# First attention's tail, routing and slots run per batch between the heads of the next batch

## What is computed

```
logits = einsum('bsh,eh->bse', x, router_w) + expert_bias
scores = softmax(logits); top_w, top_idx = top_k(scores, 4)
top_w = top_w / sum(top_w)
out = sum over the four of top_w * down[e](silu(x @ gate[e]) * (x @ up[e]))
```

## Time and profile before

| | us |
|---|---|
| median of 3 runs | 710.92 |
| profiled execution | 710.83 |
| its span in the trace | 709.0 |
| TensorE busy | 551.6 (78%) |
| VectorE busy | 366.9 (52%) |
| ScalarE busy | 231.2 (33%) |
| GpSimd busy | 266.8 (38%) |
| mean granted clock of TensorE | 0.868 |

### The profile page before, as it was taken

How to read it: one execution, slowest core, us unless ns; L and a number is a source line. 1 busy time by engine, 2 the same in 40 slices (tenths; PEclk the granted TensorE clock), 3 DMA queues, 4 the chain that set the end, 5 groups by cost and what they waited for, 6 DMA issues and landing times.

```text
span 709.0 us, 10743 instructions
## 1 busy us (share of the span) xinstructions
PE 551.6 (78%) x3351; PEld 472.6 (67%) x3351; DVE 366.9 (52%) x956; ACT 231.2 (33%) x587; POOL 266.8 (38%) x243
## 2 busy tenths in 40 slices
PE   8889885000999999700488869669999999999994
PEld 5656574000898988600354438659999999999994
DVE  4554664500344444337479986596644444444445
ACT  4643523000455555501360103313333333333334
POOL 4462110376267894077118860040314124044000
PEclk9995987555899999955599996869999999999998
DMA  8942000122266775233100003001022020100001
GB/s 260 377 135 69 0 1 1 45 104 101 78 189 188 230 234 185 83 101 101 36 0 1 0 22 113 1 1 67 1 67 68 1 68 15 51 0 0 0 0 59
DMA packets 42266, 54.12 MB, mean 76 GB/s; under 512 B 5729, under 2 KB 37234, under 8 KB 42226
## 3 DMA queue, kind: packets, MB, share of 16 engines
q1 hardware_dynamic: 25330, 32.34, 14.5%
q10 hardware_dynamic: 13536, 12.33, 5.5%
q0 software_dynamic: 3360, 8.93, 3.9%
HBM read 36.02 MB, written 17.56 MB: 76 GB/s over the span
## 4 chain that ended last, share of the span: by engine, by line
PE 65%; DVE 11%; POOL 10%; issue 5%; DMA 4%; ACT 4%; POOLq 0%; ACTq 0%; SPq 0%; DVEq 0%
PE PS L1381 45%; POOL FA L629 4%; POOL xg L601 4%; PE PS L1577 3%; DMA FA<-xg 2%; PE PS L1478 2%; PE PS L1456 2%; DVE FA L1335 2%; PE PS L1612 1%; DVE PS L1319 1%; PE PS L1552 1%; PE PS L1636 1%; POOL FA L644 1%; PE PS L1441 1%; DMA FA<-in_w0T 1%
## 5 line engine op out<-in xcount | busy, mean ns | idle before, releaser
L1381 PE MATMUL PS<-EW,XH 128*128 128x384 f32 (+2 forms) x732 | 208.4, 366 | 6.0 <-DVE SQ L1169 4.4
L1381 PEld LDWEIGHTS PS<-EW,XH 128*128 128x128 f32 x732 | 126.2, 192 | 10.4 <-DVE SQ L1169 4.7
L1381 PE MATMUL PS<-EW,XL 128*128 128x384 f32 (+2 forms) x366 | 129.1, 353 | 0.0
L1169 DVE SCALAR_TENSOR_TENSOR SQ<-SIL,CW,PS 128x96 f32<-128x96 f32 x256 | 69.0, 311 | 115.7 <-ACT SIL L772 114.6
L1381 PE MATMUL PS<-EW,EHH 128*128 128x256 f32 (+1 forms) x476 | 101.7, 289 | 0.2
L772 ACT ACTIVATE SIL<-PS 128x192 f32<-128x192 f32 x128 | 42.6, 332 | 160.7 <-PE PS L1381 160.7
L1381 PE MATMUL PS<-EW,EHL 128*128 128x256 f32 (+1 forms) x286 | 80.1, 280 | 0.0
L1381 PEld LDWEIGHTS PS<-EW,EHH 128*128 128x128 f32 (+1 forms) x476 | 78.0, 188 | 1.1 <-issue 0.6
L1381 PEld LDWEIGHTS PS<-EW,XL 128*128 128x128 f32 x366 | 70.2, 192 | 2.2
L568 POOL TENSOR_TENSOR round_mark<-round_mark 128x1 f32<-128x1 f32 x10 | 2.2, 218 | 183.2 <-PE PS L1381 131.8
L1612 PE MATMUL PS<-ident,FA 128*128 128x128 f32 x94 | 19.0, 286 | 50.1 <-DMA FA<-xg 50.1
(11 more groups left out here) (294 smaller groups left out, 1098.3 us busy)
## 6 DMA issues: line engine op xcount, KB each, us to landing
EG<-in_gateup SPq DMA_DIRECT2D x16, 448.0 KB, 4.1
xg<-EQ SPq DMA_DIRECT2D x1, 6016.0 KB, 26.0
...
```

Of the source, the lines that this page charges most:

```text
L1169: ins = dve.scalar_tensor_tensor(out=HH[:, pos % 2, h:h + W], in0=SIL[:, s, j * W:(j + 1) * W], scalar=c, in1=bank(s)[:, I + j * W:I + (j ...
L1381: ins = pe.matmul(o, l, r, start=start and i == 0, stop=stop and i == n - 1, skip_group_check=True)
```

## The change

- The steps of a finished batch run between the heads of the next one, down to its slots. The numbers in the table (`COPY_AT`, ...) are units on ScalarE and VectorE and pairs of units on TensorE; `batch_at` adds 8 units or 4 pairs per batch. The loops run over 46 units.
- ScalarE copies the turned heads and their 17th-column sums (`copies`), the denominator is folded into the head norm (h/d normalised is h times an inverse root of var(h) + eps d d), and inverse roots are made on VectorE by `rsqrt` (an integer guess and three Newton steps, 10 instructions) in place of ScalarE's square root and a reciprocal.
- The router's weights are multiplied with the output projection once (`fold_transposes`, `fold_products`, `fold_router`), and stand as 16 more columns behind its 256 (DR = 272). The logits of x come from the same PSUM bank and are corrected with mean and deviation afterwards. The softmax of all 16 is gone: the exponential is taken of the four best only.
- An expert has a region of 1024 rows in `xg`, so that a slot is 1024 e + rank and needs no count of later batches. `xg` has 16384 rows. Its zeros are written by a DMA that ScalarE issues between its two tanh, where SyncE did it before. For each tile ScalarE reads the row at which it starts from a table in registers, 16 at a time (a load and 32 register instructions, at tiles 0, 16 and 32). The output tensor `yg` stays packed; `pack_slots` makes the second set of slots for its gather.
- GpSimd scatters batch by batch, 8 indirect DMAs each. The gates are made for two tiles at once.
- The copy of an output tile moves from ScalarE to VectorE (`outputs`).

```diff
-        xg = nc.dram_tensor("xg", (SLOT_TILES * P, D), F32).ap()
+        xg = nc.dram_tensor("xg", (E0 * T, D), F32).ap()
...
-        FLOOR_AT, EVAC_AT, TOKENS_AT = 2, 1, 4
-        HEADS_AT, SQUARE_AT, SUMS_AT = (4, 5), (5, 6), (6, 7)
+        ROWS_AT_ONCE = 16
+        FLOOR_AT, FOLD_COPY_AT, FOLD_AT = 2, 4, 8
...
+        EVAC_AT, COPY_AT, DEN_AT, SCALE_AT, PARTS_AT = 9, 12, 12, 13, 15
+        NORM_AT, X_AT, TOP_AT, PICK_AT, SLOT_AT = 17, 18, 18, 19, 21
+        TOKENS_AT, TURN_AT, PROJECT_AT, RANKS_AT = 5, 7, 8, 10
+        UNITS = (B - 1) * NH0 + SLOT_AT + 1
...
-            sp.wait_ge(zero_set, 1)
-            sp.dma_start(xg.rearrange("(n p) d -> p n d", p=P),
-                         EQ[:].rearrange("p t e -> p (t e)").unsqueeze(1).broadcast_to([P, SLOT_TILES, D])
-                         ).then_inc(xg_zero, 16)
...
-            for t in range(NT):
-                pool.wait_ge(hc_ready, t + 1)
-                pool.tensor_tensor(OGATE[:, t, :], OGATE[:, t, :], HC[:, t, :], ALU.mult).then_inc(og_ready, 1)
...
+            def gate(b):
+                two = slice(2 * b, 2 * b + 2)
+                pool.wait_ge(hc_ready, b + 1)
+                pool.tensor_tensor(OGATE[:, two, :], OGATE[:, two, :], HC[:, two, :], ALU.mult).then_inc(og_ready, 1)
+            def scatter(b):
+                pool.wait_ge(x_act, 2 * b + 2)
+                pool.wait_ge(slots_ready, b + 1)
+                for t in (2 * b, 2 * b + 1):
+                    for k in range(TOP0):
+                        n = t * TOP0 + k
+                        pool.indirect_dma_start(
+                            out=xg, out_offset=bass.IndirectOffsetOnAxis(ap=slots[:, n:n + 1], axis=0),
+                            in_=XB[:, t, :], in_offset=None).then_inc(scattered, 16)
+            gate(0)
+            gate(1)
+            pool.wait_ge(xg_zero, 16)
+            scatter(0)
+            gate(2)
+            scatter(1)
+            gate(3)
             split(BGH, BGL, bg[:]).then_inc(w_split, 1)
...
+            act.wait_ge(zero_set, 1)
+            act.dma_start(xg.rearrange("(n p) d -> p n d", p=P),
+                          EQ[:].rearrange("p t e -> p (t e)").unsqueeze(1).broadcast_to([P, E0 * NT, D])
+                          ).then_inc(xg_zero, 16)
...
+            def copies(b):
+                two = slice(2 * b, 2 * b + 2)
+                if b == 0:
+                    act.wait_ge(w_split, 4)
+                if b >= 2:
+                    act.wait_ge(sq_read, b - 1)
+                act.wait_ge(ao_tokens, 2 * b + 2)
+                ao = PS[:, 6:8, :].rearrange("p t (h v) -> p t h v", h=NH0)
+                act.activation(hn[:, two, 0:NH0], ao[:, :, :, DV0], ACT.Copy)
+                act.activation(HC[:, two, :].rearrange("p t (h v) -> p t h v", h=NH0), ao[:, :, :, 0:DV0], ACT.Copy
+                               ).then_inc(hc_ready, 1)
+                s = 2 * (b % 2)
+                act.activation(SQ[:, s:s + 2, :].rearrange("p t (h v) -> p t h v", h=NH0), ao[:, :, :, 0:DV0], ACT.Square
+                               ).then_inc(sq_done, 1)
...
+            def pair_x(b):
+                for t in (2 * b + 1, 2 * b):
+                    act.wait_ge(lg_ready, 2 * b + 1 + (t % 2 == 0))
+                    act.activation(XB[:, t, :], bank(7 - t % 2)[:, 0:D], ACT.Identity, bias=nb[:, t:t + 1],
+                                   scale=rstd[:, t:t + 1]).then_inc(x_act, 1)
...
+                if i % ROWS_AT_ONCE == 0:
+                    _, at = nc.values_load_multi_w_load_instructions(tile_rows[0:1, i:i + ROWS_AT_ONCE], engines=(mybir.EngineType.Activation,),
+                                        min_val=0, max_val=E0 * NT - 1)
+                    rows.update(enumerate(at, i))
+                act.dma_start(XG[:, i % 4, :], room[bass.ds(rows[i], 1)].rearrange("o p d -> p (o d)")
+                              ).then_inc(xg_ld[i % 4], 16)
...
+            def rsqrt(x, y, a, b):
+                ch.link(dve.tensor_scalar(y.bitcast(I32), x.bitcast(I32), -0.5, 1597463007.0, ALU.mult, ALU.add))
+                for _ in range(3):
+                    ch.link(dve.tensor_tensor(a, y, y, ALU.mult))
+                    ch.link(dve.scalar_tensor_tensor(out=b, in0=x, scalar=-0.5, in1=a, op0=ALU.mult, op1=ALU.mult))
+                    ch.link(dve.scalar_tensor_tensor(out=y, in0=b, scalar=1.5, in1=y, op0=ALU.add, op1=ALU.mult))
...
+            def scale_heads(b):
+                two = slice(2 * b, 2 * b + 2)
+                v, e2 = hs[:, two, 0:NH0], hs[:, two, NH0:2 * NH0]
+                dve.wait_ge(sq_done, b + 1)
+                s = 2 * (b % 2)
+                summed = dve.tensor_reduce(v, SQ[:, s:s + 2, :].rearrange("p t (h v) -> p t h v", h=NH0), AX_X, ALU.add)
+                summed.then_inc(sq_read, 1)
+                dve.wait_ge(sq_read, b + 1)
+                ch.link(dve.scalar_tensor_tensor(out=v, in0=v, scalar=NH0 / D, in1=e2, op0=ALU.mult, op1=ALU.add))
+                y = hr[:, two, 0:NH0]
+                rsqrt(v, y, hr[:, two, NH0:2 * NH0], e2)
+                dve.wait_ge(og_ready, b + 1)
+                shape = [P, 2, NH0, DV0]
+                dve.tensor_tensor(HC[:, two, :].rearrange("p t (h v) -> p t h v", h=NH0),
+                                  OGATE[:, two, :].rearrange("p t (h v) -> p t h v", h=NH0),
+                                  y.unsqueeze(3).broadcast_to(shape), ALU.mult).then_inc(gated, 1)
...
+            def pair_norm(b):
+                two = slice(2 * b, 2 * b + 2)
+                dve.wait_ge(y_done, 2 * b + 2)
+                for t in (2 * b + 1, 2 * b):
+                    ins = dve.bn_stats(st[:, t, :], bank(7 - t % 2)[:, 0:D])
+                ch.link(ins)
+                for t in (2 * b + 1, 2 * b):
+                    ins = dve.bn_aggr(mv[:, t, :], st[:, t, :])
+                ch.link(ins)
+                ch.link(dve.tensor_scalar(rv[:, two], mv[:, two, 1], EPS_LN, None, ALU.add))
+                rsqrt(rv[:, two], rstd[:, two], t1[:, two, 0], t1[:, two, 1])
+                ch.link(dve.scalar_tensor_tensor(out=nb[:, two], in0=mv[:, two, 0], scalar=-1.0, in1=rstd[:, two],
+                                                 op0=ALU.mult, op1=ALU.mult))
+                for t in (2 * b + 1, 2 * b):
+                    ins = dve.scalar_tensor_tensor(out=LG[:, t, E0:2 * E0], in0=wr0_sum[:], scalar=nb[:, t:t + 1],
+                                                   in1=bias_r0[:], op0=ALU.mult, op1=ALU.add)
+                ch.link(ins)
+                for t in (2 * b + 1, 2 * b):
+                    dve.scalar_tensor_tensor(out=LG[:, t, 0:E0], in0=bank(7 - t % 2)[:, D:DR], scalar=rstd[:, t:t + 1],
+                                             in1=LG[:, t, E0:2 * E0], op0=ALU.mult, op1=ALU.add).then_inc(lg_ready, 1)
...
+                def outputs(v):
+                    dve.wait_ge(tiles_done, v + 1)
+                    if v >= 4:
+                        dve.wait_ge(yg_st[v % 4], 16 * (v // 4))
+                    dve.tensor_copy(YO[:, v % 4, :], bank(6 + v % 2)[:, 0:D]).then_inc(y_evac, 1)
...
-            dve.wait_ge(w_split, 3)
-            layernorm(0, XB, y_done, lambda p: 2 * p + 2)
-            lo_parts(1, XL, XH)
-            softmax(0, E0, bias_r0[:])
-            dispatch()
-            normalise(t2, top, 4, None).then_inc(weights_ready, 1)
+            dve.wait_ge(slots_ready, B)
+            dve.tensor_tensor(t1[:, :, 0:TOP0], top[:, :, 0:TOP0], top[:, :, 0:1].broadcast_to([P, NT, TOP0]),
+                              ALU.subtract).then_inc(rt_max, 1)
+            tile_tables()
+            pack_slots()
+            dve.wait_ge(rt_exp, 1)
+            normalise(t2, t3, TOP0, None).then_inc(weights_ready, 1)
...
             def heads_to_tokens(b):
                 pe.wait_ge(ao_evac, 2 * (b + 1))
-                pe.wait_ge(at_ready, 2)
-                if b >= 1:
-                    pe.wait_ge(hc_ready, b * TB)
+                if b == 0:
+                    pe.wait_ge(fold_ready, 1)
...
+            def heads_turned(b):
+                pe.wait_ge(sq_done, b + 1)
+                pe.wait_ge(gated, b + 1)
+                for k in range(KD):
+                    for t in range(2):
+                        c = (k * 2 + t) * P
+                        ins = pe.transpose(bank(6)[:, c:c + P], HC[:, 2 * b + t, k * P:(k + 1) * P], ident[:])
+                ins.then_inc(tp_done, 1)
+            def project_pair(b):
+                if b == 0:
+                    pe.wait_ge(ld_x, 16)
+                else:
+                    pe.wait_ge(slots_ready, b)
+                pe.wait_ge(lo_done, b + 1)
+                for t in (2 * b + 1, 2 * b):
+                    o = bank(7 - t % 2)
+                    c = slice(t * P, (t + 1) * P)
+                    pe.matmul(o[:, 0:D], ident[:], XA[:, t, :], start=True, stop=True, skip_group_check=True)
+                    for k in range(KD):
```

(11 more changed lines are left out.)

370 lines of the change are left out of this document (232 added, 138 removed).

## The result

The kernel became slower: 717.81 us (median of 15 runs, 712.17 to 721.84) against 713.34 us for the kernel before (15 runs, 701.72 to 719.07). The ratio is 1.0139, with a 95% interval of 1.0106 to 1.0172. A second series gave 713.58 against 704.15 and 1.0137 (1.0075 to 1.0200). All ratios here leave out executions that took over 1.5% more than the fastest of their own kernel, which in the first series are eight of the 15 of the kernel before and none of the changed one, and so its two medians, taken of all, lie only 0.6% apart. The forecast was 695, and its range ended at 714. The loss is inside what the text called no change, but both intervals lie above 1, and it is on the other side.

A forecast was written before the change was run, and what follows sets the result against it. The serial stretch from 87.3 to 179.4 us was taken as the place to win. Terms -13.9 - 30.6 + 25.3 + 3.0 = -16.2 us from 710.83 gave 694.6, said as 695; range 680 to 714.

The forecast's parts named there:

- last weights product: Last VectorE product of weights in the heads: expected to end at 112.6 us against 87.3, 25.3 us lost.
- chain to the last slots: Serial steps from the last weights product to the last batch's slots: 32 us taken against 45.9, 13.9 us won.
- 24 scatters: Scatters behind the last slots fall from 32 to 8; 24 at 1.28 us each, 30.6 us won.
- reads and landing: ScalarE's first register read of 16 tile rows, in the path behind the last scatter: 1.5 us lost.
- tiles, with two reads: Expert tiles: the two other register reads lose 1.5 us together; TensorE stays the bound.
- prologue: Before the heads: ScalarE issues the zero write between its two tanh, 0.9 us lost.
- batch 0: First batch of heads: gains four transposes and six small products for the fold, 16.3 us instead of 15.0.
- batch 1: Second batch of heads, with batch 0's denominators and scaling on VectorE: 17.5 us taken, part of it at half clock.
- R1: Rival: TensorE's clock holds at full; shorter batches and a chain of 28.8 us give 682 us; chance 0.20.
- R2: Rival: TensorE's clock stays at half; batches 2 and 3 at 29 us, chain 35.7, kernel 708 us; chance 0.15.
- R3: Rival: the zero write delays expert 2's load, hence split and first gate; 710 us, or 716; chance 0.13.
- VectorE's copies: Expert tiles: output-tile copies move to VectorE, 47 x 0.4 us; cost 0, between -2 and +2 us.

The follow-up runs named there:

- the fillers: Changed kernel plus filler TensorE products nobody reads, behind the last head: ratio 1.0131 to the kernel before; with tile rows also read one at a time, ahead: 0.9794.

## Why the prediction was wrong

Term by term, by the profiles (the changed kernel's first, in brackets the range over the kernels that leave this part as it is):

| term | forecast | measured |
|---|---|---|
| last weights product | +25.3 | +26.0 (110.5 to 115.7 against 87.3 and 88.4) |
| chain to the last slots | -13.9 | -6.3 (35.5 to 38.8 against 45.1 and 42.5) |
| 24 scatters | -30.6 | -30.9 |
| reads and landing | +1.5 | +5.4 |
| tiles, with two reads | +1.5 | +8.0 |
| behind the tiles | 0 | +7.1; +2.0 in the second profile |
| sum | -16.2 | +9.3 |

- **The scatter** was right to 0.3 us, and so was its place (eight of them behind the last slots).
- **The register reads** were the step that failed in kind. The text said that no row prices them, gave 0 to 5 us each, and took 1.5 for the first and 1.5 for the other two, because TensorE reads two such values in each tile with hardly any idle time. The nearest row was near in kind but not in number: 32 register instructions against two. A read holds ScalarE for 4.9 us, at the upper end of the bounds; it cost 5.4 in the path, and the tiles took 8.0 longer, of which 5.0 are TensorE's idle times at the two reads, some 2 more busy time (118.55 us against 115.90 in the earlier trace rows, of 748 and 745 instructions) at a lower clock, and 1.4 the late load at 280.63. With the reads one at a time and ahead, 7.6 of the 8.0 were gone. The condition that the text named, a gap of more than 3 us between landing and first load, came true. The terms 1.5 and 1.5 should have been 5.4 and 8.0: 10.4 of the miss of 25.5. The Trainium skill ("Runtime: NRT & Kernel Launch", "Instruction fetch mechanics") gives some 200 ns for each register that a load fills, of loads by the runtime; 16 of them would be an estimated 3.2 us. This trace does not bear that out for a kernel's own load from SBUF: it took 1.23 us for 16 values, and the rest of the 5.4 us went to the 32 register instructions behind it.
- **The chain** was walked through as it came: pair_norm of batch 3 runs from 144.49 to 148.84, 4.4 us for 4.1, the scaling from 131.53 to 135.25, 3.7 for 3.6. What failed is the mean taken between 28.8 at full clock and 35.7 at half. The clock was 0.50 in the first profile and 0.59 in the second, and the chain 38.8 and 37.3. With the fillers it was 33.0 at 0.86 once and 36.9 at 0.73 once. So of the 6.8 us over the 32 about half is the clock (up to 35.7), and some 3 us are in no term of the sum. Another 0.8 is a slip of boundaries: the 45.9 us of the kernel before run to the first issue of a scatter, the 32 only to the slots; slots to slots it had 45.1. Of what lies over 35.7, one part is in the timeline, a TENSOR_TENSOR of 16 columns that took 1.13 us beside GpSimd's gate (129.63 to 130.89), where the same instruction took 0.18 a batch earlier:

```profile
106.68 0.18 DVE L1078 TENSOR_TENSOR hn<-hn 128x16 f32<-128x16 f32 x1
...
129.79 1.13 DVE L1078 TENSOR_TENSOR hn<-hn 128x16 f32<-128x16 f32 x1
```

  The prediction cites the Trainium skill (SBUF — State Buffer, "Who interferes with whom") on engines that lock each other out; here it agrees, for an instruction with both inputs in SBUF. All twelve profiles with this instruction have it at 1.13 or 1.14 us beside the last gate, and at 0.17 or 0.18 in the two batches before, where it starts behind the gate's end. The squares of the inverse roots were not hit, since no gate or split ran beside them. The text had 1 us for waiting on the gate. The chain is another 7.6 of the miss.
- **The heads** ended where forecast, but by luck, since errors cancel. The sum counts batches from scores to scores (44.9 and 62.2 in the earlier trace rows). By these bounds the prologue did not lose its 0.9 us, batch 0 took 12.8 us instead of 16.3 (the clock was 1.00, where it had been 0.89), batch 1 19.2 instead of 17.5, and the third batch began at 61.8 where the sum had 64.6. The two full batches took 26.3 and 25.2 instead of 24 each. (The times 62.24 and 66.72 in the text are 62.17 and 66.65 in the earlier trace rows; their distance is the same.) The longest wait of TensorE was the named one, at the tokens' transposes for ScalarE's x, but 5.9 us instead of 2.7:

```profile
101.44 1.94 PE L1699 MATMUL PS<-ident,FA 128*128 128x128 f32 x8 [5.91 <-ACT XB L777]
```

- **The clock**, rival R1 and R2: neither held. It was 0.63 and 0.83 in the two batches, and half in the chain, where TensorE was idle for 20 of 38.8 us., with an idle time of 2.75 us just before a stretch at 0.50, were the right rows; the sum gave them too little in the chain.
- **The zero write**, rival R3: it fell. The write took 61.6 us and landed at 74.4, where the text had 65, before the first scatter at 87.4; the split of expert 2 waited 4.4 us for its load, which landed at 48.5 (the text put the turn at 50), the splits ended at 53.7, and the first gate stood at 53.8, which was ahead of where the forecast had it (55). The two loads of this expert took 7.4 and 8.6 us while the DMA engines moved 385 GB/s. That is about the 4 to 8 us that the prediction worked out by the rule of the Trainium skill (DMA: Bandwidth & Descriptors, "Issuing engines are not separate DMA queues"), and the trace agrees with it.
- **VectorE's copies**: nothing, as said.
- **Behind the tiles** the sum had nothing, and 7.1 us came. Some 5 of them are the slow waits of that one execution; the second profile has 2.0, and the two profiles of the kernel before differ by 1.5 there. The change has no part in it that shows.

Open: the spans of the changed kernel (718.3 and 712.9) and of the kernel before (709.0 and 708.1) differ by 3.9 to 10.2 us, by 4.8 in the second pair, while both ratios say some 10 us. What the kernel before saves in its executions of 700 us was seen in no profile: the two profiled ones took 710.83 and 709.9. Which idle times exactly lower the clock between the heads was not tried: no bank of PSUM was free for fillers there.
